# A bisection search over attention scores: two weight units quantised ahead of it, layer-norm moments inside it, and three of eight comparison tiles marked by GpSimd

## The reference

```python
# layer 0, attention: for each of 4 batches a 512 x 512 matrix of similarities of ctx_512
sim = einsum('bhnd,bhmd->bnm', ctx@Wq.T, ctx@Wk.T) / (sqrt(d) * H)
k = int(n * 0.3)                               # the 153rd largest of each row of 512
threshold = top_k(sim, k)[0][:, :, -1:]
A = sigmoid(sim) * (sim >= threshold)
A = (A + swap(A)) * 0.5
x = x + tanh(g) * ((1 - gamma) * layernorm(x) + gamma * A)
# layer 0, feed forward: all three weights go through _q_w
_q_w(w)   # blocks of 32: scale = 2^(floor(log2(blockmax)) - 2), then w / scale rounded to a 4-bit float
x = x + tanh(g2) * mx_linear(silu(gate(ln(x))) * up(ln(x)), w_down)
# layer 1: grouped attention and a mixture of 8 experts, top 2
```

## Time and profile before

| what | value |
|---|---|
| median of 3 runs | 1872.8 us (1871.12 to 1873.93) |
| profiled execution, its own time | 1870.53 us |
| its span in the trace | 1868.7 us |
| busy PE / DVE / ACT / POOL | 1484.8 / 1112.7 / 980.8 / 635.6 us |
| search, first mark to last decision | 41.6 to 349.6 us |

### The profile page before, as it was taken

The page is one execution under the profiler, slowest core; times in us unless marked ns, Lnnn a source line. Parts: engine busy times, 40 slices in busy tenths (PEclk is TensorE's granted clock), DMA queues, the critical chain, the costliest instruction groups (busy, mean ns, idle before and its releaser), DMA issues. The chain is left out here.

```text
span 1868.7 us, 31243 instructions
## 1 busy us (share of the span) xinstructions
PE 1484.8 (79%) x10376; PEld 777.9 (42%) x10395; DVE 1112.7 (60%) x1785; ACT 980.8 (52%) x1503; POOL 635.6 (34%) x557
## 2 busy tenths in 40 slices
PE   6666666677776775999999711899999999999994
PEld 2444455543333332444444310444444444444442
DVE  3999999788888896888886472205415140541000
ACT  4999999733232233777777440344444444444442
POOL 3000000010000000788888535435445444544432
PEclk9778777788898897999999765999999999999998
DMA  9311100000000000000000256315335151531113
GB/s 336 135 46 46 46 1 1 29 1 1 0 0 0 0 0 1 3 2 3 2 3 3 88 190 249 117 35 163 111 86 168 26 165 34 163 95 34 30 28 102
DMA packets 49246, 118.69 MB, mean 64 GB/s; under 512 B 5536, under 2 KB 5792, under 8 KB 48576
## 3 DMA queue, kind: packets, MB, share of 16 engines
q1 hardware_dynamic: 34832, 88.53, 14.0%
q0 software_dynamic: 8176, 18.65, 5.1%
q10 hardware_dynamic: 6144, 10.28, 1.8%
HBM read 84.21 MB, written 37.43 MB: 65 GB/s over the span
## 5 line engine op out<-in xcount | busy, mean ns | idle before, releaser
L1622 PE MATMUL PS<-R 128*128 (+1 forms) x1872 | 432.7, 381 | 8.3 <-issue 7.2
L1776 DVE TENSOR_SCALAR R<-wring 128x1024 f16<-128x1024 f32 x56 | 61.5, 1108 | 382.6 <-PE PS L1645 349.2
L425 ACT ACTIVATE R<-R 128x512 bf16<-128x512 f32 x448 | 278.9, 715 | 9.4 <-PE PS L445 3.9
L1622 PEld LDWEIGHTS PS<-R 128*128 128x128 f16 x1872 | 179.5, 98 | 217.6 <-issue 19.7
L445 PE MATMUL PS<-R,ident_b 128*128 128x256 bf16 (+1 forms) x1056 | 168.6, 321 | 83.1 <-ACT R L425 79.1
L1645 PE MATMUL PS<-R 128*128 (+1 forms) x936 | 214.8, 379 | 1.2 <-ACT R L1732 1.2
L1812 POOL TENSOR_TENSOR R<-R 128x512 f32<-128x512 f32 x78 | 113.3, 1453 | 292.0 <-ACT R L1720 181.0
L871 PE MATMUL PS<-R 128*128 128x512 bf16 x495 | 141.9, 436 | 78.6 <-DVE R L807 60.4
L1036 DVE TENSOR_REDUCE R<-PS 128x1 f32<-128x512 f32 x256 | 166.6, 686 | 45.2 <-PE PS L1218 42.6
L1014 POOL TENSOR_TENSOR R<-R 128x512 f32<-128x512 f32 x128 | 166.6, 1302 | 27.8 <-ACT R L1141 12.2
L1141 ACT ACTIVATE R<-PS 128x512 f32<-128x512 f32 x256 | 144.4, 598 | 41.3 <-PE PS L1232 40.8
(11 more groups left out here) (262 smaller groups left out, 2522.3 us busy)
## 6 DMA issues: line engine op xcount, KB each, us to landing
wring<-in_L_ffn_w_kernel_dram SPq DMA_DIRECT2D x48, 512.0 KB, 5.3
slot_rows<-R SPq DMA_DIRECT2D x1, 10023.0 KB, 40.3
R<-slot_rows ACTq DMA_DIRECT2D x39, 257.0 KB, 2.7
R<-in_L_ffn_w_kernel_dram SPq DMA_DIRECT2D x16, 512.0 KB, 5.6
wring<-in_L_ffn_wo_kernel_dram SPq DMA_DIRECT2D x16, 512.0 KB, 4.5
R<-in_L_ffn_wo_kernel_dram SPq DMA_DIRECT2D x16, 512.0 KB, 4.7
X<-in_x_dram SPq DMA_DIRECT2D x4, 1024.0 KB, 9.0
R<-in_L_ffn_w_up_dram SPq DMA_DIRECT2D x4, 1024.0 KB, 10.3
```

Of the source, the lines that this page charges most:

```text
L425: nc.scalar.activation(marks[:, j * S:(j + 1) * S], SIM[:, tile * S:(tile + 1) * S], ACT.Sign, bias=cfloat[:, tile:tile + 1], scale=-1.0). ...
L1622: mm = nc.tensor.matmul(bank[2 * half + g], ZT[n][:, (4 * pz + k) * P:(4 * pz + k + 1) * P], weights(place, at), start=(i % 12 == 0), stop ...
```

## The change

It moves VectorE work out of, and GpSimd work into, the search:

1. Units 0 and 1 (`EARLY = 2`) are quantised by VectorE before the search, into buffers of their own (`unit_space`); their loads are issued ahead of x, and units 2 to 5 ahead of the store of zeros. The ten other units follow half-steps 8 to 57.
2. The moments of x move from before the search into half-steps 0 to 7, two tiles each; the rest of the layer norm into half-steps 8, 10 and 12.
3. Of the 8 marks of a half-step, ScalarE now makes 5 (tiles 0 to 4), GpSimd 3 (tiles 5 to 7), VectorE none. GpSimd's 16 scalings of x go between its marks, one in every second half-step from 16.
4. `keep` and `near` become instructions with two tensor inputs (scalar_tensor_tensor and tensor_tensor) where they were tensor_scalar.
5. TensorE's transposes and ScalarE's copies of a unit follow a table, `TURN_AT`.

```diff
-ACT_MARKS = 7
+ACT_MARKS = 5
+POOL_MARKS = 3
...
+        EARLY = 2
+
+        def unit_space(u):
+            if u < EARLY:
+                return (R2[:, 8708:10756], marks_f, (R2[:, 10756:11780] if u else R3[:, 2 * UNIT:2 * UNIT + UNIT // 2]).bitcast(BF16),
+                        *(R2[:, 11780 + 64 * n:11844 + 64 * n] for n in range(4)))
...
             sp.dma_start(par[:, 4:5], gamma_raw.partition_broadcast(P)).then_inc(par_in, 16)
+            sp_weights(sp, 0, 2)
...
+        WEIGHTS_AT = 8
+        TURN_AT = [1, 3] + [WEIGHTS_AT + 5 * u + 5 for u in range(10)]
...
-                if h >= 6 and (h - 6) % 5 == 0 and (h - 6) // 5 < 11:
-                    act_weights(act, (h - 6) // 5)
-            act_weights(act, 11)
+                if h - 1 in TURN_AT:
+                    act_weights(act, TURN_AT.index(h - 1))
...
                         if q:
-                            pe.wait_ge(marked_dve, h + 1)
+                            pe.wait_ge(marked_pool, (h + 1) * POOL_MARKS)
...
-                        fold((7, 8), ident_2)
-                        mm = fold((4, 7), ident_b[:])
+                        fold((ACT_MARKS, 8), ident_2)
+                        mm = fold((4, ACT_MARKS), ident_b[:])
...
-            with v.Fori(0, NT) as t:
-                dve_moments(v, t)
-            dve_ln_var(v, 0, 0)
-            dve_ln_scale(v, 0)
...
+            for u in range(EARLY):
+                for k in range(5):
+                    dve_weights(v, u, k)
...
-            def mark(h):
-                t = h % 2 * HALF + HALF - 1
-                v.wait_ge(cand_ready, h + 1)
-                if h:
-                    v.wait_ge(fold_ps, 2 * h)
-                nc.vector.tensor_scalar(marks[:, (HALF - 1) * S:], SIM[:, t * S:(t + 1) * S], cfloat[:, t:t + 1], 0.5,
-                                        ALU.is_lt, ALU.subtract).then_inc(marked_dve, 1)
...
-                nc.vector.tensor_scalar(keep[:, g], cnt[:, g], float(S - 2 * TOPK), -1.0, ALU.is_le,
-                                        ALU.mult).then_inc(keep_step, 1)
+                nc.vector.scalar_tensor_tensor(out=keep[:, g], in0=cnt[:, g], scalar=float(S - 2 * TOPK), in1=minus,
+                                               op0=ALU.is_le, op1=ALU.mult).then_inc(keep_step, 1)
...
-                    nc.vector.tensor_scalar(near[:, g], key[:, g], bit[:, n + 2:n + 3], None,
+                    nc.vector.tensor_tensor(near[:, g], key[:, g], bit[:, n + 2:n + 3].broadcast_to([P, HALF]),
                                             ALU.bitwise_xor).then_inc(near_step, 1)
...
+            for h in range(HALVES):
                 search(h)
+                moments(h)
+                if 0 <= h - WEIGHTS_AT < 50:
+                    dve_weights(v, EARLY + (h - WEIGHTS_AT) // 5, (h - WEIGHTS_AT) % 5)
...
+        def pool_search(pool):
+            pool.wait_ge(sim_sb, NT)
+            for h in range(HALVES):
+                pool.wait_ge(cand_ready, h + 1)
+                if h:
+                    pool.wait_ge(fold_ps, 2 * h)
+                for j in range(ACT_MARKS, HALF):
+                    tile = h % 2 * HALF + j
+                    nc.gpsimd.tensor_scalar(marks[:, j * S:(j + 1) * S], SIM[:, tile * S:(tile + 1) * S],
+                                            cfloat[:, tile:tile + 1], 0.5, ALU.is_lt, ALU.subtract).then_inc(marked_pool, 1)
+                if h == NT // 2 + 2:
+                    pool_ln(pool, 0)
+                if 16 <= h < 16 + 2 * NT and h % 2 == 0:
+                    t = h // 2 - 8
+                    if t == 0:
+                        pool.wait_ge(coef_ready, 5)
+                    xt = X[:, t * D:(t + 1) * D]
+                    nc.gpsimd.tensor_scalar(xt, xt, s1[:, t:t + 1], s2[:, t:t + 1], ALU.mult, ALU.add).then_inc(lin, 1)
...
             sp_load(sp)
+            sp_weights(sp, 2, 6)
             sp_zero(sp)
-            sp_weights(sp)
+            sp_weights(sp, 6, 12)
```

More of the change, by code:

```diff
@@ L120, in bass_flamingo @@
         bit = R3[:, 5844:5876].bitcast(I32)
+        minus = R3[:, 5944:5952]
         ident_2 = R3[:, 5880:5944].bitcast(BF16)
-        marks = R3[:, 6144:8192].bitcast(BF16)
+        marks_f = R3[:, 6144:8192]
+        marks = marks_f.bitcast(BF16)
         A = R1[:, 0:8192]
@@ L129, in bass_flamingo @@
         WDT = R2[:, 8192:12288].bitcast(BF16)
[L131 to L137, removed]
+        EARLY = 2
[3 more added lines that the diff above has]
+                        *(R2[:, 11780 + 64 * n:11844 + 64 * n] for n in range(4)))
+            return (R3[:, 0:UNIT], R3[:, UNIT:2 * UNIT], R3[:, 2 * UNIT:2 * UNIT + UNIT // 2].bitcast(BF16),
+                    R3[:, 5120:5184], R3[:, 5184:5248], R3[:, 5248:5312], R3[:, 5376:5440])
         bz = R1[:, 8192:8704]
@@ L462, in pe_search @@
                     mm.then_inc(fold_ps, 1)
-                if h >= 5 and h % 5 == 0 and h <= 60:
-                    pe_weights(pe, h // 5 - 1)
+                if h in TURN_AT:
+                    pe_weights(pe, TURN_AT.index(h))
         def dve_a(v):
-            v.wait_ge(x_in, 64)
-            with v.Fori(0, NT) as t:
-                dve_moments(v, t)
-            dve_ln_var(v, 0, 0)
-            dve_ln_scale(v, 0)
+            nc.vector.memset(key, -2 ** 31).then_inc(bit_step, 1)
+            nc.vector.memset(one, 1).then_inc(bit_step, 1)
+            nc.vector.memset(cbits, 0).then_inc(bit_step, 1)
+            nc.vector.memset(minus, -1.0).then_inc(bit_step, 1)
+            for n in range(32):
+                nc.vector.memset(bit[:, n:n + 1], -2 ** 31 if n == 0 else 2 ** (31 - n)).then_inc(bit_step, 1)
+            for u in range(EARLY):
+                for k in range(5):
+                    dve_weights(v, u, k)
             v.wait_ge(tg_ready, 2)
@@ L478, in dve_a @@
             v.wait_ge(coef_ready, 3)
[L479 to L489, removed]
+            v.wait_ge(wb_ready, EARLY)
+            v.wait_ge(bit_step, 36)
             v.wait_ge(id_ready, 2)
@@ L539, in search, with moments @@
                     nc.vector.tensor_copy(near[:, g], key[:, g]).then_inc(near_step, 1)
[L541 to L549, removed]
+            def moments(h):
+                if h < NT // 2:
+                    for t in (2 * h, 2 * h + 1):
+                        if t % TPB == 0:
+                            v.wait_ge(x_in, 16 * NB)
+                        dve_moments(v, t)
+                elif h == NT // 2:
+                    for part in range(2):
+                        dve_ln_var(v, 0, part)
+                elif h == NT // 2 + 4:
+                    v.wait_ge(ln_pow, 2)
+                    nc.vector.scalar_tensor_tensor(out=nmr[:], in0=lnt[:, 0, :], scalar=-0.5, in1=rstd[:],
+                                                   op0=ALU.mult, op1=ALU.mult).then_inc(ln_ready, 1)
+                    v.wait_ge(ln_ready, 1)
+                    nc.vector.tensor_scalar(s1, rstd[:], coef[:, 0:1], 1.0, ALU.mult, ALU.add).then_inc(coef_ready, 1)
+                    nc.vector.tensor_scalar(s2, nmr[:], coef[:, 0:1], None, ALU.mult).then_inc(coef_ready, 1)
+            for h in range(HALVES):
                 search(h)
+                moments(h)
+                if 0 <= h - WEIGHTS_AT < 50:
+                    dve_weights(v, EARLY + (h - WEIGHTS_AT) // 5, (h - WEIGHTS_AT) % 5)
             nc.vector.tensor_tensor(key, key, gone, ALU.bitwise_xor).then_inc(fin_step, 1)
@@ L676, in raw_loads, with sp_weights @@
             return 16 * (1 if u < 2 else (u - 2) // 4 + 1)
-        def sp_weights(sp):
-            for u in range(12):
+        def sp_weights(sp, first, end):
+            for u in range(first, end):
                 if u >= 6:
@@ L697, in dve_weights @@
             raw_u = raw_unit(u)
+            wy, wc, wb, wam, wpow, wsc, wri = unit_space(u)
             wf = lambda c: v.wait_ge(wf_step, u * 4 + c)
@@ L728, in dve_weights @@
                 wq(4)
-                if u:
+                if u >= EARLY:
                     v.wait_ge(wtr_ps, 2 * u)
@@ L747, in pe_weights @@
             pe.wait_ge(wb_ready, u + 1)
+            wb = unit_space(u)[2]
             for h in range(2):
@@ L757, in act_weights @@
             dn = WDT.rearrange("p (c o) -> p c o", c=16)
-            if u == 0:
+            if u == 8:
                 act.wait_ge(xs_zero, 16)
@@ L1867, in _ @@
             pool_d_consts(pool)
-            pool_ln(pool, 0)
-            pool_linear(pool)
+            pool_search(pool)
             pool_b_weights(pool)
```

6 lines of the change are left out of this document (3 added, 3 removed).

## The result

The changed kernel takes 2159.9 us (median of 4 runs, 2159.0 to 2162.6) where the kernel before takes 1872.0 beside it: 1.155 times as long, 95% interval 1.152 to 1.157. The direction was forecast, the size was not: 288 us more, where 20 were.

What follows compares the result with a forecast made beforehand. VectorE was taken to set the pace, at 23.8 us a unit. Search terms 255 + 5 + 60 + 8 = 328 us against 308, plus 0.3 for the start, gave 1870.5 + 20 + 0.3 = 1891 us; range 1855 to 1925.

Steps and rivals of the forecast that it cites:

- the price of GpSimd's mark: Each of GpSimd's three marks in a half-step takes 0.764 us, as L605 does; three are 2.3 us.
- The upper bound: Top cost of a GpSimd mark, from L1820 with two tensors and a 16-bit output: 1.157 us.
- The ring of marks and folds: GpSimd's three marks, TensorE's fold and hand-overs, each waiting for the other, take 3.6 or 4.5 us a half-step.
- The rest of the sum: Search time: ten units 255 us, scalings 5, half-steps without a piece 60, around them 8; 328 us, 20 more than before.
- The hold of some 0.5 us: A GpSimd mark holds a VectorE instruction for some 0.5 us of its 0.764.
- the pace of a unit: A unit's five half-steps on VectorE take 21.8 us without its marks, 25.5 with 3.7 lost to holds; before 23.8.
- the 14 half-steps without a piece: Half-steps 0 to 7 at 4.4 us and 58 to 63 at 4.2, set by marks and folds: 60 us.
- The rival that two-input instructions pass: Two-tensor VectorE instructions are not held by GpSimd's one-input mark: 298 us of search, 1861 in all; chance 0.26.
- both kinds are held: VectorE instructions with one tensor in and with two are both held by GpSimd's marks; a unit loses 3.7 us.
- Starving: Rival: GpSimd's second and third marks wait for each long VectorE piece to end; about 2010 us, chance 0.04.
- The start: Quantising two units before the search delays its start by 0.3 us, with unit 0 landing at about 10.5 us.
- The signs named beforehand: L724 every 25.5 us, small instructions up to 0.6 us, marks near 0.76 with maxima beyond 2, TensorE waiting for GpSimd's marks.

Runs made afterwards that it cites:

- The probe: Kernel before with 14 GpSimd instructions of 128 x 512 (seven forms, two turns) added at its idle start, output unused; 1874.6 us in one run.
- e_fma: Changed kernel with GpSimd's three marks computed by mult and add instead of is_lt and subtract, finding another threshold; 1888.3 us, ratio 1.0083.
- e_nomark: Changed kernel with GpSimd's marks given back: ScalarE marks 7 tiles, VectorE 1, GpSimd none; 1876.7 us, ratio 1.0013.
- e_turn: e_nomark with the two early units' transposes and copies moved from half-steps 1 and 3 to 9 and 11; 1873.5 us, ratio 0.9997.
- e_two: e_turn with VectorE marking two tiles and ScalarE six in the fourteen half-steps without a piece; 1866.6 us, ratio 0.9963.
- e_buf1: e_pool1 with GpSimd's one mark in a two-half buffer of its own, waiting for the fold two half-steps back; 1877.6 us, ratio 1.0025.
- e_pool1: Changed kernel with ScalarE marking 7 tiles, GpSimd 1 and VectorE none; 1873.9 us, ratio 0.9999.
- e_small: Changed kernel with `keep` and `near` put back to their one-tensor form; 2163.6 us in one run.

## Why the prediction was wrong

*The step that failed* is the price of GpSimd's mark, "three marks at 0.764 (the price of L605, one tensor in, 128 x 512, two scalars)". It measured 1.99 us with nothing beside it. The row was alike in engine, size and number of inputs. It differed in the pair of operations (mult and add in L605, is_lt and subtract in the mark), in the output type and in its second scalar, and I counted none of these as a part of the price. The probe and e_fma show that the pair alone decides: the mark's own form with mult and add takes 0.69 us. The upper bound went by L1820, 1.157 us, which was too low as well, and the stated range left even that out. No tensor_scalar of GpSimd in the kernel before had another pair. Why the pair matters to GpSimd stays open.

*What it did.* The ring of marks and folds went from 3.6 to 4.5 us to 8.1, which is over any VectorE time of a half-step. 3 x (1.97 - 0.76) x 64 = 232 us is the price alone, with 1.97 from start to start. The holds of GpSimd by VectorE's long pieces (1.46 us in the half-step shown, 73 us in the whole search) lengthened the ring further, since a mark was now what all waited for. The two come to more than the loss of 285 us, since a ring of 3.6 to 4.5 us is shorter than the mean half-step before, 308 / 64 = 4.8 us. The low clock is in the ring too: the fold takes 1.9 us at it and 1.05 at the high one.

*The rest of the sum, at the price it assumed,* is tested by e_fma: 15.5 us over before measured, 20 worked out. `keep` and the candidate are held there in most half-steps (medians 0.61 and 0.58 us), `near` in few (median 0.17). The hold of some 0.5 us read from L494 and L507 was right (`keep`, 0.17 us by itself, ends 0.70 us into a mark, so it was let go at 0.53), and the pace of a unit came out as worked out, 26.1 us; the 14 half-steps without a piece were cheaper: some 59 us of the search with what stands around them, where 60 and 8 were reckoned. With a mark of 0.70 us the change is slower by 0.8%. The rival that two-input instructions pass is refuted for that mark. For the mark as it is written `keep` does pass, with 0.17 us all 64 times: the sentence "both kinds are held" does not carry over.

*Starving.* The prediction gave 2010 us to marks that wait behind every long piece, on another mechanism. The mean mark is 2.38 us, of which 0.38 is waiting: a part of the loss, not its cause.

*The start* was 2.5 us later, not 0.3: the first unit was there at 12.8 us instead of 10.5 (VectorE's first block maximum of the changed kernel, 12.85 us), and the last piece ended 3 us after the last similarity. Part of that differs from run to run: with the same start e_fma had its first unit at 11.8 us and its first mark at 43.1.

*Parts 1, 2, 4 and 5* together: I took 48 us off for two units and gave most of that back in 14 half-steps; e_nomark measured 2 to 3 us more than before, since ScalarE with seven marks sets those half-steps. That this was so was shown by e_turn and e_two, which took it from them.

*The signs named beforehand* came out in part: TensorE waited for GpSimd's marks, and marks had maxima far beyond 2 us. Of the three signs that were to make the forecast wrong, all came: the mark cost over 1 us, VectorE sat idle at the tally, and the small instructions kept to 0.2 us (`keep` in all 64 half-steps, the candidate in at least 60). No rival with a mark of 2 us had a price or a chance of its own.

## What to carry to other kernels

A price taken from a row holds for the same engine, sizes, types and also the same operations: where the new instruction differs in any of these, run it once alone before it is put on the path. An idle engine is no free engine: GpSimd's marks, even at 0.7 us, put 0.8 us between VectorE's tally and its next piece (2.25 us in the half-step shown, 1.46 before), having taken 0.40 off it. When work leaves the engine that sets the pace, look at once at the second slowest; here ScalarE's marks and copies took nearly as long, and only relieving both gave 0.4%.

## What the runs showed of the hardware

- GpSimd's tensor_scalar on 128 x 512 float32, with one scalar read from memory for each partition and one constant: mult with add 0.69 us; is_lt with subtract, subtract with min, subtract with mult, add with add 1.99 to 2.01; is_lt alone 1.57; the same for a bfloat16 and a float32 output in the two pairs tried. Other pairs were not tried.
- A mark of 2.0 us holds a small VectorE instruction no longer than one of 0.7 us does. In e_fma `keep` starts 0.09 us into a mark and ends 0.70 us into it, together with the mark. In e_buf1 `near`, also with two tensors in, starts 0.08 us into a mark of 2.0 us and ends 0.71 us into it:

```profile
162.55 2.00 POOL L617 TENSOR_SCALAR pmark<-R 128x512 bf16<-128x512 f32 x1 [0.52 <-DVE R L527]
...
162.63 0.63 DVE L533 TENSOR_TENSOR R<-R 128x8 int32<-128x8 int32 x1
```

  `keep` itself shows both: in e_pool1, at 183.10 us, it starts 0.09 us into a mark of 2.0 us and takes 0.61, and in the changed kernel it starts 0.59 us into its mark and always takes 0.17. So for instructions with two tensors in the place within the mark decides. One tensor in makes no difference at the start of a mark: L729 of the changed kernel starts 0.11 us into one, nine times, and takes 0.63 us instead of 0.20. L303, which passed under the square root, had started 1.34 us into it; the prediction read that as an instruction that lets go at once.
- Near the end of a mark of 2.0 us instructions with one tensor in are held again. In the changed kernel, at its first half-step, a mark runs from 52.46 us, `key`'s last part at 53.73 passes with two tensors in, and the candidate at 53.93, with one tensor in, is held to the mark's end:

```profile
52.46 2.00 POOL L615 TENSOR_SCALAR R<-R 128x512 bf16<-128x512 f32 x1 [2.18 <-PE PS L453]
...
53.73 0.17 DVE L518 TENSOR_TENSOR R<-R 128x8 int32<-128x8 int32 x1
53.93 0.55 DVE L520 TENSOR_SCALAR R<-R 128x8 int32<-128x8 int32 x1
```

  One pair of rows separates form from place: `near` starts 1.34 us into a mark at 453.10 us of the changed kernel, with two tensors in, and takes 0.17 us, and at 454.97 us of e_small, with one tensor in, and takes 0.68, up to the mark's end. It is a single pair.
- The same holds for one-tensor VectorE instructions on 2048 columns: L736 starts some 1.6 us into a mark and took 1.60 us in most of its runs in the search, 1.23 alone, ending later by what was left of the mark. L740, also with one tensor in, starts there no later than 1.3 us into a mark and was never held (1.22 us).
